# Two-layer graph network, one core: all node tiles of the second layer counted on chip in that layer, none counted in the first

## The reference

```python
h = relu(layernorm(x))
# layer 0: an edge network
m = silu(layernorm(concat(h[src], edge_attr) @ W1 + b1) * g1 + be1)
m = silu(m @ W2 + b2)
agg = segment_sum(m, dst)
x = x + layernorm(silu(concat(agg, h) @ Wu + bu)) * gn + bn
# layer 1: a sum over neighbours and an MLP
h = relu(layernorm(x))
agg = segment_sum(h[src], dst)
x = x + relu((h + agg) @ M1 + c1) @ M2 + c2
```

## Time and profile before

| | |
|---|---|
| median of 3 runs | 5362.1 us (5361.87 to 5362.64) |
| span of the profiled execution | 8034.5 us (no other time is given for it) |
| PE, PEld busy in that span | 4183.8, 2957.1 us |
| DVE, ACT busy | 2908.2, 2129.5 us |
| POOL busy | 3730.5 us |
| mean granted PE clock | 0.690 |
| DMA packets, data | 361343, 729.68 MB |

### The profile page before, as it was taken

The page is one execution under the profiler, slowest core; times in us unless marked ns, Lnnn a source line. Parts: engine busy times, 40 slices in busy tenths (PEclk is TensorE's granted clock), DMA queues, the critical chain, the costliest instruction groups (busy, mean ns, idle before and its releaser), DMA issues. The chain is left out here.

```text
span 8034.5 us, 84044 instructions
## 1 busy us (share of the span) xinstructions
PE 4183.8 (52%) x29487; PEld 2957.1 (37%) x29487; DVE 2908.2 (36%) x5403; ACT 2129.5 (27%) x3187; POOL 3730.5 (46%) x3907
## 2 busy tenths in 40 slices
PE   6244544354444543535444444444444475888887
PEld 5122323232222332323322232222232244777775
DVE  6243434344334443434443434443344463000001
ACT  1132323233323332323332333333232341000002
POOL 4644444545444545454444445444545404544550
PEclk8566666666666666666666666666666676888888
DMA  2122222222222222212222222222222224666663
GB/s 85 41 68 64 69 65 67 62 71 66 66 63 68 68 71 60 73 59 71 67 69 63 67 66 67 68 65 66 64 71 65 68 78 157 235 230 232 238 233 106
DMA packets 361343, 729.68 MB, mean 91 GB/s; under 512 B 156402, under 2 KB 206834, under 8 KB 350306
## 3 DMA queue, kind: packets, MB, share of 16 engines
q1 hardware_dynamic: 238338, 598.51, 20.7%
q0 software_dynamic: 122592, 125.78, 6.8%
HBM read 450.70 MB, written 273.27 MB: 90 GB/s over the span
## 5 line engine op out<-in xcount | busy, mean ns | idle before, releaser
L730 POOL DMA_INDIRECT gat<-layer_rows,idx x3752 | 3554.0, 947 | 2423.6 <-issue 1113.6
L1065 ACT ACTIVATE node_buffers<-ps 128x800 bf16<-128x800 f32 x1264 | 1058.3, 837 | 4227.7 <-remote 3224.9
L988 PE MATMUL ps<-node_buffers 64*128 64x100 bf16 x10112 | 543.1, 238 | 3005.3 <-ACT node_buffers L1065 1628.9
L988 PEld LDWEIGHTS ps<-node_buffers 64*128 64x128 bf16 x10112 | 334.5, 108 | 3636.5 <-issue 3526.0
L1139 DVE TENSOR_TENSOR edge_buffers<-ps,gat 128x512 f32<-128x512 f32 x391 | 270.2, 691 | 2797.0 <-remote 1721.9
L1187 DVE TENSOR_TENSOR node_buffers<-ps,node_buffers 128x1024 bf16<-128x1024 f32 x632 | 771.7, 1221 | 804.2 <-PE ps L988 400.4
L1666 PE MATMUL ps<-edge_buffers,node_buffers 125*128 125x192 bf16 x7900 | 833.0, 263 | 218.6 <-issue 211.3
L1666 PEld LDWEIGHTS ps<-edge_buffers,node_buffers 125*128 125x128 bf16 x7900 | 750.9, 143 | 289.0 <-issue 288.4
L756 PE MATMUL ps<-edge_buffers,w2d 128*128 128x512 f32 x782 | 640.8, 914 | 194.4 <-ACT node_buffers L766 166.1
L953 POOL DMA_INDIRECT node_buffers<-source_keys,off_i x79 | 74.9, 948 | 1360.6 <-PE ps L999 1354.1
L743 PE MATMUL ps<-w1e,edge_buffers 128*128 128x256 f32 x1564 | 618.7, 536 | 87.1 <-DVE edge_buffers L1139 49.9
(11 more groups left out here) (185 smaller groups left out, 3344.2 us busy)
## 6 DMA issues: line engine op xcount, KB each, us to landing
stored_counts<-node_buffers SPq DMA_DIRECT2D x632, 400.0 KB
node_buffers<-stored_counts SPq DMA_DIRECT2D x79, 3200.0 KB
gat<-layer_rows,idx POOLq DMA_INDIRECT x3752
edge_buffers<-in_edge_quads SPq DMA_DIRECT2D x391, 128.0 KB
node_buffers<-in_x SPq DMA_DIRECT2D x5, 625.0 KB
layer_rows<-node_buffers SPq DMA_DIRECT2D x25, 125.0 KB
residual_rows<-node_buffers SPq DMA_DIRECT2D x5, 625.0 KB
layer_rows<-node_buffers SPq DMA_DIRECT2D x5, 625.0 KB
```

Of the source, the lines that this page charges most:

```text
L730: pool.indirect_dma_start(out=gat[:, j, c, :], out_offset=None, in_=table[:, :], in_offset=bass.IndirectOffsetOnAxis(ap=idx[:, half, j, c: ...
L988: mm = pe.matmul(tp[h][:, i * T:(i + 1) * T], low_hot[node, u % PAIR_SLOTS, k, :], high_hot[node, u % PAIR_SLOTS, k, :], start=True, stop= ...
L1065: a.activation(stage[:, u % STAGES, part * GP * T:(part + 1) * GP * T].rearrange("p (i h k) -> p h i k", h=2, k=T), ps[:, 2:4, 0:4 * T].re ...
```

## The change

The first layer keeps the edge network alone: no key fetch, no one-hots of keys, no pair products, no copies and no stores of counts; `ctab` is gone. The second layer gathers no rows. It counts all 98 tiles itself, one tile ahead of the product, straight into one of two count buffers in SBUF. A pair is now one product of 128 rows and 200 columns (both nodes' keys at once, the high key of the second node shifted by T + 1), with one-hots made from bf16 constants in SBUF. ACT copies the counts out of PSUM except every fourth unit's second half, which DVE copies. In PE's order each unit's pair products are followed by an eighth of the product of the tile before. The `dst` loads and marks of the update go.

```diff
-    TILES = 79
-    T0 = NT - TILES
-    GB = 78
-    RATE = (13, 8)
...
-        PAIR_SLOTS = 4
-        low_hot = view([128, PAIR_SLOTS, GP, 128], bf16)
-        high_hot = view([128, PAIR_SLOTS, GP, T], bf16)
...
+        cnt = [view([128, GW * T], bf16) for _ in range(2)]
         raw = view([128, 3 * F])
+        PAIR_SLOTS = 3
+        low_hot = view([128, PAIR_SLOTS, GP // 2, 128, 2], bf16)
+        high_hot = view([128, PAIR_SLOTS, GP // 2, 2 * T, 2], bf16)
```

In the first layer SP's store of counts (L935 to L938), POOL's key fetch (L948 to L956), PE's `pairs` and `turn_keys`, ACT's `staged` and `copy_keys` and DVE's `mask` and `count_hots` are deleted and nothing takes their place. In the update DVE loses:

```diff
-                v.wait_ge(u_dst, 32)
-                for k in range(2):
-                    v.tensor_scalar(far[k], far[k].bitcast(i32), float(T0 * 128), float(WIN), ALU.is_ge, ALU.mult).then_inc(u_far, 1)
```

The new second layer (`mask`, `turn_keys`, `copy_keys`, `raw_sums`, `product`, `turn` do what they did, for any tile):

```diff
+        pair_banks = [ps[:, 2 * part:2 * part + 2, 0:4 * T] for part in range(2)]
+        wide = [ps[:, k, 0:3 * F] for k in (4, 5)]
+        turned = ps[0:F, 6, 0:GW]
+        key_banks = [ps[:, 7, k * 64:(k + 1) * 64] for k in range(2)]
+        LEADS = [T * i // GPS for i in range(GPS + 1)]
+        def on_vector(u, part):
+            return part == 1 and u % 4 == 3
+        def copy_counts(eng, u, part):
+            at = u % GPS * 2 * GP * T + part * GP * T
+            to = cnt[u // GPS % 2][:, at:at + GP * T].rearrange("p (b k) -> p b k", b=2)
+            wait(eng, c_use, 2 * u + part + 1)
+            wait(eng, d_sum, u // GPS - 1)
+            if on_vector(u, part):
+                return eng.tensor_copy(to, pair_banks[part])
+            return eng.activation(to, pair_banks[part], ACT.Copy)
```

POOL fetches the keys of a tile (L953's instruction) in a loop:

```diff
+                    for d in range(NT):
+                        wait(pool, c_kt, d - 1)
```

ACT's order:

```diff
+                    copy_keys(0)
+                    for d in range(NT + 1):
+                        if d > 1:
+                            raw_sums(d - 2)
+                        for i in range(GPS):
+                            if d < NT:
+                                u = d * GPS + i
+                                for part in range(2):
+                                    if not on_vector(u, part):
+                                        copy_counts(a, u, part).then_inc(c_copy[part], 1)
+                            if i == 4 and d + 1 < NT:
+                                copy_keys(d + 1)
```

PE's pair products and its order:

```diff
+                def pairs(u, part):
+                    wait(pe, c_hot, u + 1)
+                    wait(pe, c_copy[part], u)
+                    for i in range(4):
+                        k = part * 4 + i
+                        mm = pe.matmul(pair_banks[part][:, i // 2, i % 2 * 2 * T:(i % 2 + 1) * 2 * T],
+                                       low_hot[:, u % PAIR_SLOTS, k // 2, :, k % 2], high_hot[:, u % PAIR_SLOTS, k // 2, :, k % 2],
+                                       start=True, stop=True)
+                    mm.then_inc(c_use, 1)
...
+                    turn_keys(0)
+                    for d in range(NT + 1):
+                        for i in range(GPS):
+                            if d < NT:
+                                for part in range(2):
+                                    pairs(d * GPS + i, part)
+                            if i == 3 and d + 1 < NT:
+                                turn_keys(d + 1)
+                            if d > 0:
+                                product(d - 1, LEADS[i], LEADS[i + 1])
+                            if i == 1 and d > 1:
+                                turn(d - 2)
+                    turn(NT - 1)
```

DVE's one-hots and its order:

```diff
+                def count_hots(u):
+                    wait(v, c_kc, 2 * (u // GPS) + 2)
+                    wait(v, c_use, 2 * (u - PAIR_SLOTS) + 2)
+                    v.tensor_tensor(low_hot[:, u % PAIR_SLOTS, :, :, :], iol[:, :, :].unsqueeze(1).broadcast_to([128, GP // 2, 128, 2]),
+                                    spread(low_key, u, 128), ALU.is_equal)
+                    v.tensor_tensor(high_hot[:, u % PAIR_SLOTS, :, :, :], ioh[:, :, :].unsqueeze(1).broadcast_to([128, GP // 2, 2 * T, 2]),
+                                    spread(high_key, u, 2 * T), ALU.is_equal).then_inc(c_hot, 1)
...
+                    for d in range(NT + 1):
+                        for i in range(GPS):
+                            u = d * GPS + i
+                            if u + 2 < NT * GPS:
+                                count_hots(u + 2)
+                            if d < NT and on_vector(u, 1):
+                                copy_counts(v, u, 1).then_inc(c_copy[1], 1)
+                            if i == 0 and d + 1 < NT:
+                                mask(d + 1)
+                            if i == 2 and d > 1:
+                                add_tile(d - 2)
```

More of the change, by code:

```diff
@@ L934, in step @@
                         load_edges(sp, n, s, g_ea[s])
-                    for u in units_at(e, j, STORE):
-                        at = u % GPS * 2 * GP * T
-                        wait(sp, c_copy, 2 * u + 2)
-                        sp.dma_start(ctab[u // GPS, :, at:at + 2 * GP * T], stage[:, u % STAGES, :]).then_inc(c_st[u % STAGES], 16)
                 with sp.If(flagged(sp) == 0):
-                    rounds(step, STORE + 3)
-                    for k in range(STAGES):
-                        sp.wait_ge(c_st[k], 16 * sum(u % STAGES == k for u in range(UNITS)))
+                    rounds(step, 0)
             @block.gpsimd
@@ L1011, in step @@
                     edges(e, j + EARLY)
-                    units = units_at(e, j, COUNT)
-                    for u in units[0:1]:
-                        pairs(u, 0)
                     s, n = lagged(e, j, TURN)
@@ L1020, in step @@
                         transposes(pe, s, zp[1]).then_inc(g_t, 1)
-                    for u in units[0:1]:
-                        pairs(u, 1)
                     s, n = lagged(e, j, BACK)
@@ L1028, in step @@
                         back_transposes(pe, (j - BACK) % 2).then_inc(g_bt, 1)
-                    for u in units[1:2]:
-                        pairs(u, 0)
                     s, n = lagged(e, j, SECOND)
@@ L1036, in step @@
                         second_products(pe, s).then_inc(g_m, 1)
-                    for u in units[1:2]:
-                        pairs(u, 1)
-                    b = tile_at(e, j, KEYS_TURN)
-                    if b is not None:
-                        turn_keys(b)
                 with pe.If(flagged(pe) == 0):
@@ L1093, in step @@
                         messages(a, s).then_inc(g_msg, 1)
-                    for u in units[0:1]:
-                        staged(u, 1)
                     s, n = lagged(e, j, FEAT)
@@ L1561, in _ @@
             def _(sp):
-                with sp.If(flagged(sp) == 0):
-                    load_counts(sp, 0)
-                for k in range(2):
-                    sp.dma_start(far[k].bitcast(i32).rearrange("p (n c) -> p n c", c=BC),
-                                 dst[:, k * (GB // 2):(k + 1) * (GB // 2), :]).then_inc(u_dst, 16)
                 def chunk(g):
@@ L1649, in _, with turn_keys @@
+                    raw_sums(NT - 1)
             @block.tensor
             def _(pe):
-                def sums(n):
-                    j = n % UN
-                    wait(pe, g_gat[j], rows_of_first_layer(j) + (n // UN + 1) * 16 * BC)
-                    wait(pe, k_oh, n + 1)
-                    wait(pe, k_add, n)
-                    window_sums(pe, j, gat[:, j, :, :], agl).then_inc(k_sum, 1)
+                def turn_keys(d):
+                    wait(pe, c_msk, d + 1)
+                    wait(pe, c_kc, 2 * d)
+                    for k in range(2):
+                        for h in range(2):
+                            mm = pe.matmul(key_banks[k][h * 64:(h + 1) * 64, :], node_keys[:, d % 2, :, k],
+                                           identb[:, h:128:2], start=True, stop=True)
+                    mm.then_inc(c_kt, 1)
@@ L1726, in build_gnn @@
+                    add_tile(NT - 1)
         general(1, htab)
```

260 lines of the change are left out of this document (55 added, 205 removed).

## The result

The changed kernel takes 6019.1 us (median of 4 runs, 6014.9 to 6023.0) beside 5362.4 us for the kernel before: ratio 1.119, 95% interval 1.112 to 1.125, **657 us slower**. Forecast were 5990 us. One thing is needed to read all that follows: the time of these kernels differs between the chips they ran on, and each repeats its own. On some chips the kernel before takes 5362 to 5428 us, on others 7899 or 8061 us, in profiled and unprofiled executions alike, and its first profile (8034.5 us) looks like those of the second kind.

A forecast was written before the change was run, and what follows sets the result against it. The prediction took POOL's gather issue to bound the first layer, TensorE and POOL alike the second (TensorE after the change). Terms: 198 + 3882 + 70 + 157 + 1562 + 122.5 = 5991 us; range 5720 to 6240 us.

The forecast's parts named there:

- The stall: First layer: TensorE all but stops and ACT waits 27.6 us during gathers; taken as absent from timed runs.
- the rebuilt run: Kernel before without stalls, all stages: 198 + 4009 + 105 + 157 + 800 + 122.5 = 5391 us, 0.5% above the median.
- First layer, -98 us: POOL in the first layer: 79 key fetches at 1.241 us go, so 3980 us becomes 3882 us.
- The cover: First layer: eight gathers' 9.9 us a block hide the other engines' work; TensorE at most 7.5 us without counts.
- Emptying and update, -35 and 0 us: First layer's pipeline empties in 70 us instead of 105; the node update gains nothing, 157 us.
- Second layer, +762 us: Second layer counts 98 tiles itself at 15.8 us a tile: 1562 us, from 800.
- A weight read with a step of two elements costs nothing there: TensorE's second-layer pair products: stepped operands add no time, on a row of 20 of 98 columns in 1.11 us.
- The estimate from the Trainium skill: Second-layer pair products: about 90 ns at 200 columns, a tile 0.2 us longer, the sum 22 us higher.
- my loop: Second layer: second half of pairs waits for ACT's copies, 1.91 us a unit, binding in 5 of 8, 0.9 us.
- rival C: Second layer: DVE is the bound, 16.5 to 18 us a tile, total 6060 to 6200 us; chance 0.10.
- D: Second layer: the change doesn't get the faster one-hots, 25 us a tile, total 6900 us; chance 0.03.
- rival B: Second layer: TensorE doesn't hold its clock; 6165 us at 0.87, 6390 us at 0.75; chance 0.14.

The follow-up runs named there:

- before_again: The kernel before, unaltered, profiled on a quick chip: 5366.6 us (5362.0 to 5427.4); the profiled execution took 5427 us.
- counts_in_both_2: Changed kernel with the whole counting of 79 tiles put back into the first layer, its results unread: 6147 us beside 6025 us for the changed kernel.
- all_act: Changed kernel, its own order of work, with all count copies on ACT, none on DVE: 6805 us beside 8061 us for the kernel before.
- halves_all_act: Changed kernel with half of each unit's product between the halves of its pairs and all count copies on ACT: 6754 us where the kernel before takes 8061.
- few_products: Changed kernel with 9 of the 100 products of each second-layer tile left, all else kept: 5898.5 us (5866.3 to 5923.6).

## Why the prediction was right, and where not

**The stall.** "I take the stall for a cost of recording" is the step that failed. before_again was recorded and has no stall; on the chips of the 7899 and 8061 us the traces have it, and the unrecorded executions there are as long as the recorded ones. The argument against the 6240 us first layer (3831 issues at 1.25 us fill 89% of the timed run) was sound, and so the rebuilt run was: stage by stage 201, 4008, 80, 156, 821 and 159 us (the last some 60 less in executions of 5365 us) against 198, 4009, 105, 157, 800 and 122.5. Right was the choice of base, wrong the reason, and with it the sentence that the changed kernel's record should still hold stalls. The reason mattered: with "a cost of recording" the forecast holds everywhere, with "a condition of some chips" it holds only for chips of the first kind.

**First layer, -98 us.** Measured -103.6 us (4007.1 to 3903.5), that is 1.25 us a fetch and 5 us more. The cadence is 1.248 to 1.250 us in both kernels; the 1.241 us that the prediction fitted to the median was a little low. The cover held: TensorE was busy 56% of the stage, at a granted clock of 0.72.

**Emptying and update, -35 and 0 us.** From the last gather to the start of the update, the emptying went from 80.6 us (4208.4 to 4289.0) to 53.3 us (4104.9 to 4158.2), -27 us. Both terms of the forecast were too long, 105 and 70 us: the 105 us came from the profile with the standing engines. The update took 156.7 us (4289.0 to 4445.7, the second layer's first product) and takes 157.3 us (4158.2 to 4315.5, its first key fetch): nothing, as forecast. counts_in_both_2 agrees, with 82.3 us of emptying (4200.4 to 4282.7) and 157.1 us of update (4282.7 to 4439.8).

**Second layer, +762 us.** Measured 1589 us (first key fetch 4315.5 to last product 5904.8) less 810 us, +779 us. The tile is 16.06 us and not 15.8. TensorE's own work is 15.3 us, not 14.9: a pair product takes 0.091 us and not 0.0865 (64 are 0.3 us more), of which the step of two elements is 0.005. "A weight read with a step of two elements costs nothing there" rested on a row of 98 columns where nothing was compared; the row couldn't carry it. The estimate from the Trainium skill (page TensorE: Matmul & The Clock Gate, section Back-to-back issue gap), 90 ns at 200 columns, comes near the 91 ns here by luck, since that figure holds the step: without it 200 columns take 86 ns, and 192 columns 83 ns where the estimate has 89. What lay between TensorE and the tile, 0.9 us by my loop, is 0.76: a wait of 0.18 to 0.19 in four of eight units, not five. It is not DVE's copies that spare the others, as the loop had it: all_act takes them away, and the waits stay four a tile. halves_all_act gives 0.46 us of it back, which shows that it was waiting for copies.

**DVE.** 14.5 us a tile forecast, 14.5 us in few_products. The one-hots took 0.695 and 0.984 us (0.68 and 0.98 forecast). So rival C was 1.6 us away, and D did not come.

**The clock.** 0.99 over the second layer, with waits of 0.2 us every second unit: rival B did not come. The rule of the Trainium skill on that rival (page TensorE: Matmul & The Clock Gate, section A second HAM failure mode: psum-queue depth-cycling) did not apply to idles of this size.

Sum by the measured steps: -104 - 27 + 0 + 779 = 648 us of the 657 measured. The other 9 us were not found: the final network of an execution of 5362 us was never profiled.

The forecast of 5990 us lies 29 us under the measured 6019 us. Its reasons held: the bound of each layer, and what the change does to it. That the saving of 133 us came out at 131 is in part luck, since the first layer gave 6 us more than forecast and the emptying 8 us less; the added work was taken 17 us too low.

## What to carry to other kernels

Work that lies beside a bound engine is nearly free until it is moved to a stage where its own engines are the bound: the counting of 79 tiles costs 122 us beside the first layer's gathers, 98 of them for issues on the bound engine itself, and the second layer that does it for 98 tiles, with faster one-hots, is 779 us longer. That price holds where it was measured: on a slow chip the same counting costs some 1585 us, so measure both kernels in one place, and in more than one place, before keeping either. If a profiled execution is much longer than the timed ones, rebuild the timed run from the cadence of its bound engine, but profile again elsewhere before giving the difference a name. And where two engines alternate through PSUM, put work between the two halves of one engine's share; here that gave 26 us, and 44 with the copies on one engine, where the copies on one engine alone gave 3.

## What the runs showed that I had not expected

**Chips.** The kernel before takes 5362 to 5428 us on three occasions, 7899 and 8061 us on two, each repeated within 1.3%; the difference lies only in stretches with gathers (first to last gather of the changed kernel 3904 us against 4613 to 4618 and 4651 to 4661 us; granted clock 0.72 against 0.65).

**The last stage's clock.** The kernel before has two times on the quick chips, about 5365 and 5425 us. The profile of a run with the longer one shows TensorE at half clock through the final network, behind a second layer at 1.00:

```profile
5230.00:5250.00 20.00, 20.00 (x229) 19.42 (x228) 1.19 (x6) 0.66 (x2) 1.89 (x2) 1.00 0.28 116
...
5270.00:5300.00 30.00, 25.88 (x75) 11.31 (x73) 3.34 (x8) 9.63 (x15) 0.00 (x0) 0.51 0.40 91
5300.00:5350.00 50.00, 41.77 (x119) 19.05 (x121) 6.69 (x16) 13.48 (x21) 0.00 (x0) 0.50 0.11 24
```

The stage takes 159 us so and 103 us in the changed kernel, which had 0.98 there; the 56 us between them are near the 60 us between the two times. No execution with the shorter time was profiled, so that its last stage ran at full clock is inferred. What makes it fall was not tested.
